# Sorting 400,000 edges to their nodes: first segments of 2 and 6 chunks, both folded beside a third of 66

## The chip, the core and the metric

The kernel runs on one core of a Trainium2 chip. The metric is the device time of one execution in microseconds (us), smaller is better. Before the change the median of three runs is 4207.56 us (4206.01 to 4213.95).

## What is computed

A graph has 12,500 nodes (64 features each) and 400,000 edges (32 features each). Each edge belongs to one source node. Per node the kernel needs the sum, the maximum and the mean of its edges' features; then a small network of two layers runs on them and its result is added to the node's own features. Cut to that:

```python
seg_sum = jax.ops.segment_sum(edge_attr, row, num_segments=N)
seg_max = jax.ops.segment_max(edge_attr, row, num_segments=N)
cnt = jax.ops.segment_sum(jnp.ones((edge_attr.shape[0], 1)), row, num_segments=N)
seg_mean = seg_sum / jnp.maximum(cnt, 1.0)
seg_max = jnp.where(cnt > 0, seg_max, 0.0)
h = jnp.concatenate([seg_sum, seg_max, seg_mean, u[batch]], axis=1)
return x + (jax.nn.relu(h @ W1 + b1) @ W2 + b2)
```

`row` (called `src` in the kernel) is drawn at random, so a node's edges lie anywhere in the list.

## The kernel before

**Chunks and groups.** The edges lie as 128 partitions by 3125 columns. 25 columns are a chunk (125 chunks), 5 columns a group (5 groups in a chunk, 625 in all). One indirect DMA on POOL (line 439) sends one column, 128 edge rows of 128 bytes, to their places in a DRAM array `sorted_rows`; so there are 3125 of them.

**Planes and ranks.** `sorted_rows` is made of planes. A plane has one row for each node (12,544 rows of 128 bytes, 1568 KB). The first edge of a node in a segment goes to the segment's first plane (rank 0), the second to the next one, and so on. Planes have to hold zeros before edges are sent to them; each is zeroed by one DMA (`fill`, line 309), 110 in all. The rank of every edge comes out of matmuls: TensorE compares the edges of a column with one another and keeps a running count (lines 460, 473, 476, 500, 504, 506), ScalarE copies between PSUM and SBUF (lines 615, 623, 636, 638), VectorE builds the one-hot matrices (line 721), picks each edge's rank out (line 730) and writes `position` (line 742), on which POOL waits. The DVE writes the position of a group only when the same group of the chunk before has been sent (`edges_sent`), so it can be about one chunk ahead of POOL and no further.

**Segments.** `SEGMENTS` lists (chunks, ranks, parts). The chunks are cut into six segments with planes of their own. When all edges of a segment are sent, its planes are *folded*: read back as windows of 14 blocks of nodes (two halves of 7 blocks), summed over the ranks by TensorE (`sum_ranks`, line 531, one f32 matmul for each rank and half) and reduced to their maximum by VectorE (`raise_half` and `take_ranks`: line 779 makes a mask of ranks that a node does not have, line 784 adds it, 4 times in a chunk, line 801 takes the maximum rank by rank). There are 7 windows (`ROUNDS`), and a segment's ranks may be cut into parts; each window and part is worked on beside one chunk of the next segment. So 36 ranks in 3 parts are 21 chunks with 12 ranks each, and in the program a loop of 7 turns with a body of 3 chunks. Segments of 1 part are a loop of 7 turns with one chunk each. The last segment is folded at the end, with nothing beside it.

**Order.** `run_chunks` (line 283) lays the same order out for each engine: for each segment some lead chunks, then the chunks with a fold beside them, then the rest. The lead is 3 chunks on TensorE, ScalarE and VectorE and 1 on SP. In its chunk SP issues in this order: for each of the 5 groups the load of the group's edge features (`load_group`, 80 KB, line 313), after waiting until the same group of the chunk before was sent; behind it the plane fills that the chunk has; behind groups 2 and 4 a window half (`load_half`, line 319), after waiting that TensorE and VectorE are done with the half before (lines 359 and 360). All of these go through one hardware queue, first in, first out.

**What POOL waits for.** For each group: `position_ready` and `edges_loaded` of that group. At the start of segments 0 to 3: that the planes which the segment can reach are zeroed (`first_filled`, 8 planes, ahead of everything; `early_filled`, 18 planes, ahead of chunk 4; `middle_filled`, 48, ahead of chunk 17; `late_filled`, 36, ahead of chunk 74). Chunk 0 has no fills, chunks 1 to 17 have 6 each.

```python
SEGMENTS = [(4, 8, 1), (13, 14, 1), (57, 36, 3), (24, 18, 2), (17, 15, 1), (10, 12, 1)]
```

If a node had more edges in a segment than it has ranks, the whole would be done a second time for the edges left over (`passes_i`).

Of the kernel before, what the change touches and what calls it, by code (L numbers as in the profile page):

```python
# [17 lines left out]
SEGMENTS = [(4, 8, 1), (13, 14, 1), (57, 36, 3), (24, 18, 2), (17, 15, 1), (10, 12, 1)]  # L18
BLOCKS = 98
# [5 lines left out]
FILLS = 6  # L25
FILL_CHUNKS = 17
PLANES = BASE[1] + FILLS * FILL_CHUNKS
assert BASE[-1] <= PLANES


def build(nc, x, src, edge_attr, u, w1, b1, w2, b2, out, rows):
# [24 lines left out]
    EARLY, MIDDLE, REMAIN = 3 * FILLS, 8 * FILLS, 6 * FILLS  # L56
# [9 lines left out]
    for s in range(1, SEGS):  # L66
        assert SEGMENTS[s][0] >= LEAD + ROUNDS * parts[s - 1]

    assert first[1] == 4 and first[1] + 1 + ROUNDS * parts[0] <= 13 and first[2] == 17
# [12 lines left out]
    PAIRS = ROUNDS * sum(parts)  # L82
    last_steps = 4 + len(levels(depth[LAST]))
# [10 lines left out]
    with ctx:  # L94
# [46 lines left out]
        left_t = sb("left_t", [P, BLOCKS], FP32)  # L141
# [135 lines left out]
        def pair_at(s, q, r, j):  # L277

            return (s, q * PAIRS + (r * parts[s] + (pair_base[s] + j)), r * 2, j * depth[s],
                    q * STEPS + (r * (parts[s] * pair_steps[s]) + (step_base[s] + j * pair_steps[s])))  # L280

        def run_chunks(eng, q, lead, chunk):


            for s in range(SEGS):
                a, z = first[s], first[s + 1]
                ahead = lead if s > 0 else 1
                for c in range(a, a + ahead):
                    chunk(q * CHUNKS + c, c, c * GROUPS, s, None)
                a += ahead  # L290
                if s > 0:
                    k = parts[s - 1]
# [11 lines left out]
        def _(sp):  # L304
# [27 lines left out]
            with sp.Fori(0, end) as q:  # L332
# [9 lines left out]
                def chunk(c, at, n, s, pair):  # L342
                    done = early_filled if s == 0 else \
                        middle_filled if s == 1 and (n is not None or pair is not None) else \
                        late_filled if s == 1 or (s == 2 and (n is not None and n < (FILL_CHUNKS + 1) * GROUPS)) else None
                    if n == 0:
                        done = None
                    for k in range(GROUPS):
                        if n != 0:
                            sp.wait_ge(edges_sent[k], c * (16 * GROUP))  # L350
                        load_group(c, at, k)
                        if done is not None:
                            fill(at * FILLS + (BASE[1] - FILLS + k), done)
                            if k == GROUPS - 1:
                                fill(at * FILLS + (BASE[1] - 1), done)
                        if pair is not None and k in (2, 4):
                            of, p, f, r, _ = pair
# [89 lines left out]
        def _(pe):  # L447
# [5 lines left out]
            with pe.Fori(0, end) as q:  # L453
# [70 lines left out]
                def sum_ranks(pair, h, a, z):  # L524
                    s, p, _, _, _ = pair
                    if a == 0:
                        pe.wait_ge(win_loaded[h], p * 16 + 16)
                        pe.wait_ge(left_step, q * (3 * SEGS) + (3 * s + 3))
                        pe.wait_ge(sum_folded, p * 2 + (h + 2))
# [158 lines left out]
        def _(dve):  # L688
# [28 lines left out]
            with dve.Fori(0, end) as q:  # L717
# [28 lines left out]
                def take_counts(s):  # L746
                    done = q * (3 * SEGS) + 3 * s
                    dve.wait_ge(count_turned, q * SEGS + (s + 1))
                    nc.vector.tensor_scalar(left_t[:, :], count_ps, -float(BASE[s]), None, ALU.add).then_inc(left_step, 1)
                    dve.wait_ge(left_step, done + 1)  # L750
                    nc.vector.tensor_tensor(left_sum[:, :], left_sum[:, :], left_t[:, :], ALU.add)
                    nc.vector.reduce_max(most_s[:, :], left_t[:, :], axis=AXIS_X).then_inc(left_step, 1)
# [23 lines left out]
                def raise_part(s, h, col, r, a, z, steps):  # L776
# [3 lines left out]
                                            left_t[:, bass.ds(col, SLOTS)].unsqueeze(1).to_broadcast([P, z - a, SLOTS]),  # L780
# [45 lines left out]
                def chunk(c, at, n, s, pair):  # L826
                    for g in range(GROUPS):
                        if pair is not None and g in (2, 4):
                            _, p, f, _, _ = pair
# [5 lines left out]
                        of, p, f, r, steps = pair  # L835
# [108 lines left out]
```

## Time and profile before

| | us |
|---|---|
| median of three runs | 4207.56 (4206.01 to 4213.95) |
| the profiled execution, its own time | 4215.91 |
| its span | 4214.1 |
| POOL busy | 3051.1 (72%) |
| TensorE matmul / VectorE / ScalarE busy | 2943.5 / 2484.8 / 1832.9 |
| moved by DMA | 454.49 MB, 108 GB/s over the span |

The span in 40 slices of 105 us, busy tenths of each engine, the granted TensorE clock in tenths of full speed, and what the DMA engines moved:

```profile
PE   5676668876666666666666677778776777768746
DVE  5466448853333333333333378888875777658876
POOL 5777777777777777777777777777777777777720
PEclk8578558865555555555555588888877888768867
GB/s 296 335 378 380 344 263 117 118 26 26 25 26 25 26 26 25 26 25 26 26 25 26 64 112 117 106 113 109 111 60 78 92 85 94 56 92 123 91 117 100
```

The first six slices are those with plane fills. Slices 7 and 8 have the fold of segment 1, slices 23 to 29 that of segment 2, 31 to 35 that of segment 3, 36 to 38 that of segment 4; the last two are the last fold and the network. POOL shows the same digit throughout: it issues its indirect DMAs one behind the other, and what it needs between two of them is not counted as busy.

### The profile page before, as it was taken

The page shows a single profiled execution, that of the slowest core. Times are in us where ns is not written, and L with a number is a line of the kernel's source. Part 1 is how long each engine was busy: PE and PEld are TensorE (multiplying, and loading weights), DVE is VectorE, ACT ScalarE, POOL GpSimd, SP SyncE. Part 2 cuts the span into 40 slices and gives each one's busy share as a digit, 9 for nine tenths or more (in the row PEclk, how much of TensorE's full clock was granted, in tenths as well). Part 3 has the DMA queues.
Part 4 walks back from the last instruction along what each step waited for, and adds up shares of the span by engine and source line. Part 5 has one row for each costly group of instructions (what it writes and reads, how often), then busy time and mean ns, then how long its engine had stood idle before and what let it go on. Part 6 is the DMA issues. An engine that isn't in the chain of part 4 may idle for free.

```text
span 4214.1 us, 86474 instructions
## 1 busy us (share of the span) xinstructions
PE 2943.5 (70%) x19960; PEld 2213.6 (53%) x19960; DVE 2484.8 (59%) x10168; ACT 1832.9 (43%) x5899; POOL 3051.1 (72%) x3143
## 2 busy tenths in 40 slices
PE   5676668876666666666666677778776777768746
PEld 3455446654444444444444466666665665556635
DVE  5466448853333333333333378888875777658876
ACT  4444443454444444444444444444444444443424
POOL 5777777777777777777777777777777777777720
PEclk8578558865555555555555588888877888768867
DMA  7899874311111111111111234333322333234333
GB/s 296 335 378 380 344 263 117 118 26 26 25 26 25 26 26 25 26 25 26 26 25 26 64 112 117 106 113 109 111 60 78 92 85 94 56 92 123 91 117 100
DMA packets 410045, 454.49 MB, mean 108 GB/s; under 512 B 65002, under 2 KB 381460, under 8 KB 409620
## 3 DMA queue, kind: packets, MB, share of 16 engines
q1 hardware_dynamic: 309876, 401.37, 29.0%
q0 software_dynamic: 100000, 51.40, 5.0%
q14 instruction: 128, 1.05, 0.1%
q8 instruction: 41, 0.67, 0.1%
HBM read 221.50 MB, written 231.02 MB: 107 GB/s over the span
## 4 chain that ended last, share of the span: by engine, by line
POOL 47%; issue 21%; DVE 12%; PE 10%; DMA 7%; ACT 1%; POOLq 1%; SPq 1%; DVEq 1%; ACTq 0%
POOL sorted_rows L439 47%; DVE peak_ps L801 4%; DMA sorted_rows<-edges,position 4%; PE misc_ps L531 3%; DVE raised L784 3%; DMA edges<-in_edge_attr 2%; PE start_ps L500 2%; PE place_ps L504 1%; DVE picked L730 1%; PE same_ps L473 1%; PE place_ps L506 1%; DVE hot_owner L721 1%; DVE raised L812 1%; ACT start_sb L615 1%; PE same_ps L476 1%
## 5 line engine op out<-in xcount | busy, mean ns | idle before, releaser
L439 POOL DMA_INDIRECT sorted_rows<-edges,position x3125 | 3042.3, 974 | 983.0 <-issue 968.7
L504 PE MATMUL place_ps<-start_sb,lent 98*128 98x128 bf16 x3125 | 857.2, 274 | 979.4 <-DVE rank_f L730 978.0
L615 ACT ACTIVATE start_sb<-start_ps 98x128 bf16<-98x128 f32 x3125 | 867.5, 278 | 1207.9 <-PE place_ps L506 586.5
L730 DVE CUSTOM_DVE_ANT_0 picked<-place_ps,hot_owner 128x128 bf16<-128x128 f32 x3125 | 864.5, 290 | 407.9 <-PE place_ps L506 353.1
L500 PE MATMUL start_ps<-hot_owner,hot_block 128*98 128x128 bf16 x3125 | 942.7, 302 | 178.5 <-ACT start_sb L615 134.9
L504 PEld LDWEIGHTS place_ps<-start_sb,lent 98*128 98x128 bf16 x3125 | 391.1, 125 | 1075.4 <-DVE rank_f L730 1056.9
L506 PE MATMUL place_ps<-hot_owner,lent 128*128 128x128 bf16 x3125 | 870.7, 279 | 0.0
L500 PEld LDWEIGHTS start_ps<-hot_owner,hot_block 128*98 128x98 bf16 x3125 | 469.9, 150 | 756.9 <-ACT start_sb L615 639.9
L742 DVE SCALAR_TENSOR_TENSOR position<-rank_c,src_f 128x5 int32<-128x5 f32 x625 | 104.3, 167 | 1188.3 <-DMA sorted_rows<-edges,position 1148.7
L476 PE MATMUL same_ps<-lent 98*128 98x128 bf16 x3125 | 702.4, 283 | 0.0
L636 ACT ACTIVATE lent<-hot_t_ps 98x256 bf16<-98x256 bf16 x625 | 239.6, 383 | 1027.5 <-PE hot_t_ps L460 1025.0
L531 PE MATMUL misc_ps<-win,ident_f 128*128 128x224 f32 x2548 | 641.4, 410 | 0.0
L460 PE MATMUL hot_t_ps<-ident_b,hot_block 128*98 128x128 bf16 x3125 | 619.2, 273 | 24.2 <-DVE hot_owner L721 23.3
L531 PEld LDWEIGHTS misc_ps<-win,ident_f 128*128 128x128 f32 x2548 | 556.9, 228 | 18.8
L623 ACT ACTIVATE lent<-same_ps 128x512 bf16<-128x512 f32 x1250 | 541.7, 433 | 0.3
L473 PE MATMUL same_ps<-later_b,ident_b 128*128 128x512 bf16 x1250 | 515.8, 413 | 0.0
L460 PEld LDWEIGHTS hot_t_ps<-ident_b,hot_block 128*98 128x98 bf16 x3125 | 411.9, 167 | 35.3 <-DVE hot_owner L721 24.4
L476 PEld LDWEIGHTS same_ps<-lent 98*128 98x128 bf16 x3125 | 387.5, 133 | 0.8 <-issue 0.8
L506 PEld LDWEIGHTS place_ps<-hot_owner,lent 128*128 128x128 bf16 x3125 | 386.2, 124 | 0.0
L784 DVE SCALAR_TENSOR_TENSOR raised<-peak_ps,win 128x1344 f32<-128x1344 f32 (+2 forms) x252 | 376.3, 1493 | 8.7
L801 DVE TENSOR_TENSOR peak_ps<-raised,peak_ps 128x448 f32<-128x448 f32 x525 | 329.8, 628 | 16.2
L721 DVE TENSOR_TENSOR hot_owner<-owner,iota_b 128x640 bf16<-128x640 bf16 x625 | 305.5, 489 | 0.0
(80 smaller groups left out, 1725.5 us busy)
## 6 DMA issues: line engine op xcount, KB each, us to landing
sorted_rows<-zeros SPq DMA_DIRECT2D x110, 1568.0 KB, 17.3
win<-sorted_rows SPq DMA_DIRECT2D x56, 1344.0 KB
edges<-in_edge_attr SPq DMA_DIRECT2D x625, 80.0 KB
sorted_rows<-edges,position POOLq DMA_INDIRECT x3125
win<-sorted_rows SPq DMA_DIRECT2D x28, 1008.0 KB
win<-sorted_rows SPq DMA_DIRECT2D x14, 1680.0 KB
win<-sorted_rows SPq DMA_DIRECT2D x14, 1568.0 KB
win<-sorted_rows SPq DMA_DIRECT2D x14, 896.0 KB
```

What stands on the lines that cost most here:

```text
L439: nc.gpsimd.indirect_dma_start(out=rows[:, :], out_offset=bass.IndirectOffsetOnAxis(ap=position[:, t:t + 1], axis=0), in_=edges[:, k, j * ...
L460: last = nc.tensor.transpose(hot_t_ps[0:BLOCKS, j * P:(j + 1) * P], hot_block[:, slot * GROUP + j, :], ident_b[:, :])
L473: nc.tensor.matmul(same_ps[:, a * P:z * P].rearrange("p (j m) -> p j m", m=P), ident_b[:, :], later_b[:, :].unsqueeze(1).to_broadcast([P, ...
L476: last = nc.tensor.matmul(same_ps[:, j * P:(j + 1) * P], hot, hot, start=False, stop=j in (BANK_TILES - 1, GROUP - 1), skip_group_check=True)
L500: nc.tensor.matmul(start_ps[0:BLOCKS, 0:P], hot_block[:, t, :], hot_owner[:, t, :], start=False, stop=False, skip_group_check=True).then_i ...
L504: nc.tensor.matmul(place_slot(j), hot_block_t[:, slot, j * P:(j + 1) * P], start_sb[:, j, :], start=True, stop=False)
L506: nc.tensor.matmul(place_slot(j), earlier[:, slot, j * P:(j + 1) * P], hot_owner[:, t, :], start=False, stop=True).then_inc(place_ready, 1)
L531: last = nc.tensor.matmul(side_sums[h], ident_f[:, :], win[:, h, r, :], start=(r == 0), stop=(r == depth[s] - 1))
L615: nc.scalar.activation(start_sb[:, j, :], start_ps[0:BLOCKS, 0:P], ACT.Copy)\
L623: nc.scalar.activation(earlier[:, slot, a * P:z * P], same_ps[:, a * P:z * P], ACT.Relu)\
L730: nc.vector.tensor_tensor_reduce(out=picked[:, j, :], in0=place_slot(j), in1=hot_owner[:, t, :], scale=1.0, scalar=0.0, op0=ALU.mult, op1= ...
L784: return nc.vector.scalar_tensor_tensor(raised[:, h, a:z, :].rearrange("p r (b f) -> p r b f", f=FEAT), mask.unsqueeze(3).to_broadcast([P, ...
```

## The change

It does four things. (1) The first segments get 2 chunks with 6 ranks and 6 chunks with 9, and the third 66 chunks with 39 ranks, 13 in each of its 3 parts; segments 3 to 5 begin at the same chunks as before (74, 98, 115) with the same ranks. (2) Nothing is folded beside segments 0 and 1. Both are folded beside segment 2: segment 0 beside chunks 9 to 15 and segment 1 beside chunks 16 to 22 in SP's order, two chunks later on the others; for this the count table `left_t` gets two buffers. (3) Chunks 0 to 7 have 7 fills each, the first of them in chunk 0 right behind its edge loads; chunks 8 to 15 have 6 each. (4) The waits follow: 6 planes ahead of everything, 14 more ahead of chunk 2, 42 more ahead of chunk 8, 48 ahead of chunk 74. There are 110 fills as before. The ranks to fold are 99 instead of 103.

```diff
-SEGMENTS = [(4, 8, 1), (13, 14, 1), (57, 36, 3), (24, 18, 2), (17, 15, 1), (10, 12, 1)]
+SEGMENTS = [(2, 6, 1), (6, 9, 1), (66, 39, 3), (24, 18, 2), (17, 15, 1), (10, 12, 1)]
+
+BESIDE = [[], [], [0, 1], [2], [3], [4]]
...
-FILLS = 6
-FILL_CHUNKS = 17
-PLANES = BASE[1] + FILLS * FILL_CHUNKS
-assert BASE[-1] <= PLANES
+FILLS = (7, 6)
+FILL_CHUNKS = (8, 8)
+PLANES = BASE[1] + FILLS[0] * FILL_CHUNKS[0] + FILLS[1] * FILL_CHUNKS[1]
+assert BASE[-1] - 1 <= PLANES
...
-    EARLY, MIDDLE, REMAIN = 3 * FILLS, 8 * FILLS, 6 * FILLS
+    EARLY, MIDDLE, REMAIN = 2 * FILLS[0], 6 * FILLS[0], 8 * FILLS[1]
...
-        left_t = sb("left_t", [P, BLOCKS], FP32)
+        left_t = sb("left_t", [P, 2, BLOCKS], FP32)
...
-                ahead = lead if s > 0 else 1
+                ahead = lead if BESIDE[s] else 1
...
-                if s > 0:
-                    k = parts[s - 1]
+                for of in BESIDE[s]:
+                    k = parts[of]
                     with eng.Fori(0, ROUNDS) as r:
                         for j in range(k):
-                            chunk(q * CHUNKS + (r * k + (a + j)), r * k + (a + j), None, s, pair_at(s - 1, q, r, j))
+                            chunk(q * CHUNKS + (r * k + (a + j)), r * k + (a + j), None, s, pair_at(of, s, q, r, j))
...
                     for k in range(GROUPS):
                         if n != 0:
                             sp.wait_ge(edges_sent[k], c * (16 * GROUP))
                         load_group(c, at, k)
-                        if done is not None:
-                            fill(at * FILLS + (BASE[1] - FILLS + k), done)
-                            if k == GROUPS - 1:
-                                fill(at * FILLS + (BASE[1] - 1), done)
+                        for i in range(k, fills, GROUPS):
+                            fill(at * fills + (base + i), done)
...
                 def turn_counts(s):
-                    if s > 0:
-                        pe.wait_ge(sum_folded, q * (PAIRS * 2) + (pair_base[s] * 2 + 2))
+                    if pairs_before[s] > 0:
+                        pe.wait_ge(sum_folded, q * (PAIRS * 2) + (pairs_before[s] * 2 + 2))
```

SP at the start of the program. `zeros` are the plane fills, `in_edge_attr` the edge loads of chunk 0. Before:

```order
L309 DMA sorted_rows<-zeros 256x1x1568 x8
L313 DMA edges<-in_edge_attr 128x160 x5
L298 UNCONDITIONAL_BRANCH
L298 ISA
L313 ISA
```

And now:

```order
L313 DMA sorted_rows<-zeros 256x1x1568 x6
L317 DMA edges<-in_edge_attr 128x160
L313 DMA sorted_rows<-zeros 256x1x1568 x2
L317 DMA edges<-in_edge_attr 128x160
L313 DMA sorted_rows<-zeros 256x1x1568 x2
L317 DMA edges<-in_edge_attr 128x160
L313 DMA sorted_rows<-zeros 256x1x1568
L317 DMA edges<-in_edge_attr 128x160
L313 DMA sorted_rows<-zeros 256x1x1568
L317 DMA edges<-in_edge_attr 128x160
L313 DMA sorted_rows<-zeros 256x1x1568
```

Two fills fewer stand ahead of the first edge load, and two stand between the first and the second, and between the second and the third.

VectorE in a chunk with a fold of segment 2 beside it, the two instruction pairs of one half of a window (mask, then mask and window to `raised`). Before:

```order
L784 SCALAR_TENSOR_TENSOR raised<-peak_ps,win 128x1344
L792 REGISTER_ALU
L779 TENSOR_TENSOR peak_ps<-left_t,iota_f 128x42
L783 REGISTER_ALU
L784 SCALAR_TENSOR_TENSOR raised<-peak_ps,win 128x1344
```

And now:

```order
L785 SCALAR_TENSOR_TENSOR raised<-peak_ps,win 128x1344
L793 REGISTER_ALU
L780 TENSOR_TENSOR peak_ps<-left_t,iota_f 128x49
L784 REGISTER_ALU
L785 SCALAR_TENSOR_TENSOR raised<-peak_ps,win 128x1568
```

The second of the two is one rank (224 elements) longer; behind them one more maximum of 128x448 (line 801, now 802) is taken in each chunk, 12 where there were 11, and TensorE adds up 13 ranks of each half where there were 12.

## Rows read from the trace of the kernel before

**Rows 1.** The page, its line of busy engines (us, share of the span).

```profile
PE 2943.5 (70%) x19960; PEld 2213.6 (53%) x19960; DVE 2484.8 (59%) x10168; ACT 1832.9 (43%) x5899; POOL 3051.1 (72%) x3143
```

**Rows 2.** Page, group of line 439; POOL's timeline (start, us): first two, last.

```profile
L439 POOL DMA_INDIRECT sorted_rows<-edges,position x3125 | 3042.3, 974 | 983.0 <-issue 968.7
...
41.14 1.12 POOL L439 DMA_INDIRECT sorted_rows<-edges,position  x1 [31.55 <-issue]
42.57 0.96 POOL L439 DMA_INDIRECT sorted_rows<-edges,position  x1 [0.30 <-issue]
...
4033.93 0.96 POOL L439 DMA_INDIRECT sorted_rows<-edges,position  x1 [0.30 <-issue]
```

**Rows 3.** Stretches: PE, PEld, DVE, ACT, POOL busy, clock, DMA share, GB/s.

```profile
10.00:34.00 24.00, 9.42 (x63) 7.00 (x63) 17.69 (x30) 12.31 (x22) 0.00 (x0) 1.00 1.02 423
300.00:400.00 100.00, 70.16 (x518) 55.26 (x516) 68.90 (x268) 42.86 (x140) 75.94 (x79) 0.85 1.02 381
1000.00:1100.00 100.00, 65.51 (x430) 45.45 (x431) 39.53 (x224) 44.72 (x142) 75.94 (x80) 0.52 0.11 26
```

**Rows 4.** Start: SP's fills, the chain's last fill to landing, DVE's first position.

```profile
4.74 12.37 SPq L309 DMA_DIRECT2D sorted_rows<-zeros  x8
...
13.35 26.43 DMA sorted_rows<-zeros
...
33.59 0.17 DVE L742 SCALAR_TENSOR_TENSOR position<-rank_c,src_f 128x5 int32<-128x5 f32 x1
```

**Rows 5.** The page's DMA issues (size of each).

```profile
sorted_rows<-zeros SPq DMA_DIRECT2D x110, 1568.0 KB, 17.3
...
edges<-in_edge_attr SPq DMA_DIRECT2D x625, 80.0 KB
...
win<-sorted_rows SPq DMA_DIRECT2D x14, 896.0 KB
```

**Rows 6.** Chain: an edge load, issue to landing; POOL's first DMA of chunk 12.

```profile
402.67 15.52 DMA edges<-in_edge_attr
...
423.65 0.96 POOL L439 DMA_INDIRECT sorted_rows<-edges,position  x1 [0.30 <-issue]
```

**Rows 7.** Stretches of line 742 alone: start:end, length, busy (x positions), clock, DMA.

```profile
2438.20:3121.54 683.34, 17.54 (x105) 0.84 0.37 107
2633.92:2729.42 95.50, 2.54 (x15) 0.88 0.39 113
2923.62:3022.60 98.98, 2.48 (x15) 0.81 0.38 110
661.58:866.35 204.77, 5.12 (x30) 0.83 0.37 107
3788.02:3994.12 206.10, 5.01 (x30) 0.88 0.38 113
```

**Rows 8.** From the start: positions made (line 742), indirect DMAs issued (line 439).

```profile
0.00:2438.30 2438.30, 63.44 (x381) 0.60 0.35 116
0.00:3090.10 3090.10, 80.10 (x481) 0.65 0.35 115
...
0.00:2461.00 2461.00, 1841.24 (x1901) 0.61 0.34 116
0.00:3102.30 3102.30, 2330.22 (x2401) 0.65 0.35 114
```

**Rows 9.** SP's timeline, the issues ahead of chunk 96.

```profile
3084.24 0.38 SPq L319 DMA_DIRECT2D win<-sorted_rows  x1
3085.12 6.83 SPq L313 DMA_DIRECT2D edges<-in_edge_attr  x3
```

**Rows 10.** ScalarE's timeline at the top of the loop of 3 chunks.

```profile
2635.92 0.28 ACT L615 ACTIVATE start_sb<-start_ps 98x128 bf16<-98x128 f32 x1 [2.98 <-issue]
```

**Rows 11.** DVE groups in 2460 to 3100 us, by form.

```profile
L801 DVE TENSOR_TENSOR peak_ps<-raised,peak_ps 128x448 f32<-128x448 f32 x198 | 124.4, 628 | 6.1
L784 DVE SCALAR_TENSOR_TENSOR raised<-peak_ps,win 128x1344 f32<-128x1344 f32 x78 | 121.5, 1558 | 2.7
```

More of the change, by code:

```diff
@@ L66, in build @@
     for s in range(1, SEGS):
-        assert SEGMENTS[s][0] >= LEAD + ROUNDS * parts[s - 1]
-    assert first[1] == 4 and first[1] + 1 + ROUNDS * parts[0] <= 13 and first[2] == 17
+        assert SEGMENTS[s][0] >= LEAD + ROUNDS * sum(parts[j] for j in BESIDE[s])
+    assert first[1] == 2 and first[2] == 8 and SP_LEAD + ROUNDS * parts[0] == 8
+    assert BASE[2] - 1 <= BASE[1] + EARLY and BASE[3] - 1 <= BASE[1] + EARLY + MIDDLE
     DEPTH = max(depth)
@@ L82, in build @@
     PAIRS = ROUNDS * sum(parts)
+    pairs_before = [ROUNDS * sum(parts[j] for k in range(s + 1) for j in BESIDE[k]) for s in range(SEGS)]
     last_steps = 4 + len(levels(depth[LAST]))
@@ L275, in end_pass, with pair_at @@
             eng.sem_inc(pass_seen, 1)
-        def pair_at(s, q, r, j):
-            return (s, q * PAIRS + (r * parts[s] + (pair_base[s] + j)), r * 2, j * depth[s],
+        def pair_at(s, host, q, r, j):
+            return (s, host, q * PAIRS + (r * parts[s] + (pair_base[s] + j)), r * 2, j * depth[s],
                     q * STEPS + (r * (parts[s] * pair_steps[s]) + (step_base[s] + j * pair_steps[s])))
@@ L342, in chunk @@
                 def chunk(c, at, n, s, pair):
[L343 to L347, printed above, removed]
+                    done, fills, base = (early_filled, FILLS[0], BASE[1]) if s == 0 else \
+                        (middle_filled, FILLS[0], BASE[1]) if s == 1 else \
+                        (late_filled, FILLS[1], BASE[1] + (FILLS[0] - FILLS[1]) * FILL_CHUNKS[0]) \
+                        if s == 2 and (n is not None or (pair is not None and pair[0] == 0)) else (None, 0, 0)
                     for k in range(GROUPS):
@@ L351, in chunk @@
                         load_group(c, at, k)
-                        if done is not None:
-                            fill(at * FILLS + (BASE[1] - FILLS + k), done)
-                            if k == GROUPS - 1:
-                                fill(at * FILLS + (BASE[1] - 1), done)
+                        for i in range(k, fills, GROUPS):
+                            fill(at * fills + (base + i), done)
                         if pair is not None and k in (2, 4):
-                            of, p, f, r, _ = pair
+                            of, _, p, f, r, _ = pair
                             h = k // 2 - 1
@@ L524, in sum_ranks @@
                 def sum_ranks(pair, h, a, z):
-                    s, p, _, _, _ = pair
+                    s, host, p, _, _, _ = pair
                     if a == 0:
                         pe.wait_ge(win_loaded[h], p * 16 + 16)
-                        pe.wait_ge(left_step, q * (3 * SEGS) + (3 * s + 3))
+                        pe.wait_ge(left_step, q * (3 * SEGS) + 3 * host)
                         pe.wait_ge(sum_folded, p * 2 + (h + 2))
@@ L748, in take_counts @@
                     dve.wait_ge(count_turned, q * SEGS + (s + 1))
-                    nc.vector.tensor_scalar(left_t[:, :], count_ps, -float(BASE[s]), None, ALU.add).then_inc(left_step, 1)
+                    nc.vector.tensor_scalar(left_t[:, s % 2, :], count_ps, -float(BASE[s]), None, ALU.add).then_inc(left_step, 1)
                     dve.wait_ge(left_step, done + 1)
-                    nc.vector.tensor_tensor(left_sum[:, :], left_sum[:, :], left_t[:, :], ALU.add)
-                    nc.vector.reduce_max(most_s[:, :], left_t[:, :], axis=AXIS_X).then_inc(left_step, 1)
+                    nc.vector.tensor_tensor(left_sum[:, :], left_sum[:, :], left_t[:, s % 2, :], ALU.add)
+                    nc.vector.reduce_max(most_s[:, :], left_t[:, s % 2, :], axis=AXIS_X).then_inc(left_step, 1)
                     dve.wait_ge(left_step, done + 2)
@@ L779, in raise_part @@
                     nc.vector.tensor_tensor(mask,
-                                            left_t[:, bass.ds(col, SLOTS)].unsqueeze(1).to_broadcast([P, z - a, SLOTS]),
+                                            left_t[:, s % 2, bass.ds(col, SLOTS)].unsqueeze(1).to_broadcast([P, z - a, SLOTS]),
                                             iota_f[:, r + a:r + z].unsqueeze(2).to_broadcast([P, z - a, SLOTS]),
@@ L828, in chunk @@
                         if pair is not None and g in (2, 4):
-                            _, p, f, _, _ = pair
+                            _, _, p, f, _, _ = pair
                             h = g // 2 - 1
@@ L834, in chunk @@
                             continue
-                        of, p, f, r, steps = pair
+                        of, _, p, f, r, steps = pair
                         col, half = f * SLOTS, depth[of] // 2
```

## The prediction

> **What bounds the kernel now.** I read the busy engines first, then POOL's own timeline, then stretches of it, and last what stands ahead of POOL at its start and in the folds. POOL is busy 72% [rows 1], no more than TensorE, but its indirect DMAs have 0.96 us each and 0.30 us of issue between two, and nothing else: the first starts at 41.14, the last at 4033.93 [rows 2]. That is 3992.8 us for 3124 steps, 1.278 each. A quiet stretch has 79 or 80 of them in 100 us [rows 3], so 1.267 each, 6.33 a group, 31.7 a chunk, and 3124 such steps would be 3958. POOL never stalls for long: the 35 us over that are DMAs somewhat longer than 0.96 us beside folds, and one at the end. So the time is 41.1 of start, 3993 of POOL, and 180 us behind its last DMA (last fold, network). A change counts if it moves POOL's first DMA, makes POOL stall, or alters the tail. All else is cover, and the question is how thick the cover is.
>
> **Terms.** The sum is made against the profiled execution (4215.91, span 4214.1), which is 8.35 above the median of the runs; I put the difference onto the median.
>
> *The start.* POOL waits for the planes of segment 0, its first edge load and its first position. The eighth fill lands at 13.35 + 26.43 = 39.78 [rows 4], and POOL starts 1.36 later; I take 1.1 of that for the wake, the edge load of 80 KB [rows 5] landing in between at about 40.0. While only fills run, 423 GB/s are moved [rows 3], so a plane of 1568 KB (1.606 MB) [rows 5] takes 3.80. Six planes are in place at 39.78 - 7.60 = 32.2, the first load at 32.4, which would let POOL go at 33.5. The first position is written at 33.59 to 33.76 [rows 4], so it now comes last, and POOL starts at about 34.0. **-7.1.**
>
> *Fills between the edge loads of chunk 0.* The queue is first in, first out. The second load stands two planes behind the first: 2 x 3.80 + 0.3 = 7.9, landing 40.3, usable 41.4, and POOL wants it at 34.0 + 6.33 = 40.3: it stalls 1.1. For the third there are two planes again, now beside POOL's rows. In the busiest stretch the queue moves 381 GB/s [rows 3], a plane in 4.21: 8.6 more, usable at 50.0, wanted at 47.7: 2.3. Behind the fourth and fifth only one plane each, 4.4 against 6.33: no stall. **+3.4** (nothing at least, if the queue overlaps more; 5 at most). The Trainium skill, "DMA: Bandwidth & Descriptors", section "Where 436 GB/s comes from", gives 435 GB/s as the ceiling of the fabric. By that a plane is an estimated 3.7 us throughout, the term 2.1 and the sum 10.0 instead of 11.3; the trace reaches 423 with fills alone but 381 once rows and windows are in the mix, and I go by the trace.
>
> *Chunks 1 to 15.* A chunk with 7 fills moves 7 x 1.606 + 0.41 of edges in + 0.41 of rows out = 12.06 MB, at 381 GB/s 31.7 us: just POOL's pace. Before, the chunks with a fold of 8 ranks beside 6 fills moved 9.63 + 1.84 (two halves of 896 KB [rows 5]) + 0.82 = 12.29 MB, 32.3 us, and what was left at their end was this: a load issued at 402.67 landed at 418.19 and its chunk's first DMA started at 423.65 [rows 6], 5.5 us of slack, still no stall. The new chunks 9 to 15 (6 fills, 6 ranks) move 11.8 MB. The backlog therefore stays, but doesn't grow. The 14 early planes: 8 of the first 20 are done by 39.8, 12 x 4.21 and 10 loads (2 us) end at about 92.4, and POOL reaches chunk 2 at 34.0 + 63.4 + 3.4 = 100.8. The 42 next ones end 190 us later, at about 282, chunk 8 starts at 291. **0** (0 to +3). What covers this is 8 us; if it goes, POOL stalls by what is missing, and once only.
>
> *Folds of segments 0 and 1*, 6 and 9 ranks a chunk where 8 and 14 were. The one with 14 took 204.77 / 6 = 34.1 us a chunk on the DVE [rows 7] against POOL's 32.0 and ate the lead for 7 chunks, but never all of it. Less work there gives nothing. **0.** The folds as a whole have 4 ranks fewer, and that is hidden too.
>
> *The fold of segment 2*, 21 chunks, 13 ranks instead of 12. This is the large term. Look at who is ahead of whom. The 381st position (chunk 76, first group) is written by 2438.3, and POOL's DMA 1901, which uses it, starts just before 2461.0 [rows 8]: a lead of 22.5. The 481st (chunk 96) is written by 3090.1, DMA 2401 starts just before 3102.3: 12.0. Ten microseconds went in 20 chunks: the DVE needs 683.34 / 21 = 32.54 a chunk there [rows 7], POOL 32.07 (641.4 for 20). The edge loads are as close: SP sits behind its wait for TensorE, issues a window half of 12 ranks (1.5 times the 896 KB [rows 5] of 8 ranks) at 3084.24 and only then the loads for chunk 96 [rows 9], which land some 5 us later, about 3090.5; less 1.1 of wake some **10 us** are left.
>
> What does one more rank cost a chunk? In itself on the DVE: one maximum, 0.63 and a gap of 0.03, and one rank in each half of `raised`, 2 x 1.558 / 6 = 0.52 [rows 11]: 1.18. The DVE is in the chain in these steps, so little of it hides. From whole chunks: with 14 ranks 34.13, with 15 ranks 206.10 / 6 = 34.35, in loops of one chunk. The 12-rank loop has a body of 3, and at its top ScalarE loses 2.98 us that nothing shown explains [rows 10], 1.0 a chunk; the one-chunk loops have no such gap. So 12 ranks are 32.54 - 1.0 = 31.54 and a rank is (34.13 - 31.54) / 2 = 1.30. Bounds: without that correction 0.80; against the quickest turns, 95.50 / 3 - 1.0 = 30.8, it is 1.66. I take 1.25, between the two that agree. In 20 chunks 25 us are wanted and 10 are there: **POOL stalls 15 us** in the last third of the fold (ends: 6 and 23). When the fold is over the lead is rebuilt, but what POOL has lost stays lost, because POOL is the bound.
>
> *Segments 3 to 5 and the tail*: same chunks, ranks and code. **0.** The 15-rank fold keeps its thin lead.
>
> Sum: -7.1 + 3.4 + 0 + 15 = **+11.3**. On the median 4218.9.
>
> **Rivals.**
>
> *The clock favours the new fold.* Same code, same ranks: a turn of three chunks takes 95.50 at a granted clock of 0.88 and 98.98 at 0.81 [rows 7]. Which level a turn gets is not fixed by the program's text: three of the seven were quick. If all seven were quick with 13 ranks: 95.5 + 3.75 = 99.3 against POOL's 96.2, 3.0 a turn, 21 us for a lead of 19 to 22: stall 0 to 2. Then -7.1 + 3.4 + 1 = -2.7, **4204.9**, not slower: this is the case on the other side, and it decides at about 99.0 us a turn. For it: the 15-rank fold ran at 0.88 throughout; against it: the 14-rank fold had 0.83 with more ranks than 12. The Trainium skill, "TensorE: Matmul & The Clock Gate", section "Part 1: The HAM clock gate", says that the default is throttled and activity releases it; by it one more f32 matmul in each half speaks for this rival, the rows above only for half of it. Chance 0.27.
>
> *The slow clock throughout.* 99.0 + 3.75 = 102.7, 6.5 a turn, 46 in seven less 19: stall 26, **4230**. Chance 0.12.
>
> *The queue is the bound in the first chunks.* If 7 fills a chunk take 32.3 us as the heaviest chunks of before, each of chunks 1 to 7 adds up to 0.6 behind a cover that chunk 0 has used up: +4 on top of the forecast, 4223. For it: the DMA share is 1.02 already [rows 3]. Chance 0.08.
>
> *It gains its start and nothing is taken back.* A rank hides altogether, and the loads of chunk 0 come in time: -7.1, **4200.5**. Chance 0.05. *It doesn't do what it says*: a node with more edges than ranks would cost a second pass, some 4000 us. In the reference's draw the fullest node has 5, 8 and 37 edges in the three new segments, for 6, 9 and 39 ranks. Chance nil.
>
> **Numbers.** Forecast (stall between 8 and 22) 0.48. A measurement of this kernel tells about 0.2% from no change, 8.4 us: faster is below 4199.1, slower above 4216.0. Within the forecast a stall under 12.1 us still reads as no change, a quarter of it: slower 0.36 + 0.12 + 0.08 = 0.56, same 0.12 + 0.27 + 0.02 = 0.41, faster 0.03, the start's gain with a fortunate clock. The range goes from the case without a stall, 4200, to the upper bound of a rank with the queue's 3 us, 4207.6 - 3.7 + 23 + 3 = 4230, and some way into the slow clock with it: 4235. The likeliest case's own range is 4212 to 4226.
>
> **What would show it.** Right: POOL's first DMA near 34, DMA 26 (chunk 1) near 69 instead of 73.4; gaps of some us in POOL's row only between 2850 and 3130; turns of three chunks on the DVE of 99 to 103 us; SP's loads of those chunks landing as POOL wants them. Wrong: turns of 99 or less and POOL without gaps (a rank hides, or the clock); POOL's chunk 1 at 73 (the fills ate the start); gaps before 300 us (the queue); another length behind POOL's last DMA than 180.

## The result, and the profile after

The changed kernel takes 4232.07 us (median of five runs, 4230.23 to 4238.99) against 4207.56: a ratio of 1.0061, 95% interval 1.0049 to 1.0073, or 24.5 us more. The forecast had been 4218.9 (11.3 us more) in a range of 4200 to 4235. So the sign and the range held, but less than half of the rise was forecast, and 4232 lies above the likeliest case's own range of 4212 to 4226. The profiled execution took 4231.62 with a span of 4229.2, on its own median.

The page of the changed kernel: its busy engines, the moved GB/s in 40 slices of 105.7 us, the shares of the chain by engine, POOL's group (us in all, mean ns | idle time before) and the plane fills (KB each, median us from issue to landing).

```profile
PE 2943.9 (70%) x19848; PEld 2210.3 (52%) x19848; DVE 2448.5 (58%) x10140; ACT 1834.1 (43%) x5899; POOL 3038.8 (72%) x3143
...
GB/s 394 390 375 370 365 94 94 36 25 26 26 25 26 26 26 25 26 26 25 26 26 26 85 112 110 109 108 109 113 80 75 94 85 94 55 91 124 91 120 97
...
POOL 45%; issue 20%; DVE 11%; DMA 11%; PE 9%; ACT 1%; POOLq 1%; SPq 1%; DVEq 1%; ACTq 0%
...
L440 POOL DMA_INDIRECT sorted_rows<-edges,position x3125 | 3029.9, 970 | 1010.0 <-issue 964.9
...
sorted_rows<-zeros SPq DMA_DIRECT2D x110, 1568.0 KB, 14.7
```

The busy times tell nothing: VectorE's fell by 36 us [rows 1] while the kernel became 24.5 slower, and POOL's group is 12 us less busy and 27 us more idle [rows 2]. One has to look at where POOL stood idle. POOL's timeline (start, duration, in brackets the idle time before it): start, the third group of chunk 0, the last DMA ahead of the first stall beside the fold and the one behind it, a stall one turn later, and the last DMA.

```profile
34.78 1.12 POOL L440 DMA_INDIRECT sorted_rows<-edges,position  x1 [25.21 <-issue]
...
50.28 0.96 POOL L440 DMA_INDIRECT sorted_rows<-edges,position  x1 [2.83 <-issue]
...
2755.62 0.96 POOL L440 DMA_INDIRECT sorted_rows<-edges,position  x1 [0.30 <-issue]
2759.89 0.96 POOL L440 DMA_INDIRECT sorted_rows<-edges,position  x1 [3.31 <-DMA edges<-in_edge_attr]
...
2865.21 0.95 POOL L440 DMA_INDIRECT sorted_rows<-edges,position  x1 [3.21 <-DMA edges<-in_edge_attr]
...
4048.57 0.96 POOL L440 DMA_INDIRECT sorted_rows<-edges,position  x1 [0.30 <-issue]
```

Between the two profiled executions the 15.1 us of span come together like this (each rounded), taken from the starts of POOL's first DMA of a chunk: start -6.4 (41.14 to 34.78), chunk 0 +2.5 (32.3 to 34.8), chunks 1 to 15 +2.3, chunks 16 to 24 -2.3 (288.9 to 286.6), the quiet chunks 25 to 73 -6.0 (1556.5 to 1550.5), chunks 74 and 75 -0.3, **the 21 chunks beside the fold of segment 2 +25.1** (673.5 to 698.6), all later chunks together -0.4 and the tail +0.5. The -2.3 and most of the -6.0 belong to that one execution of before, not to the change: another profile of before has 286.2 in chunks 16 to 24 and 1553.0 in the quiet ones. The quiet chunks take 1550.3 to 1554.1 in eleven of the twelve profiles of the experiments and 1557.5 in the last. With the other profile's values in these two stretches the sum is +21.3, near the +24.5 of the medians; what makes the last 2.5 us of the quiet chunks is not known.

The fold of segment 2 on VectorE: two turns of three chunks and all seven, then the quiet chunks (start:end, length, busy PE, PEld, DVE, ACT, POOL, granted clock, DMA share, GB/s).

```profile
2528.88:2631.87 102.99, 80.26 (x563) 65.60 (x562) 83.84 (x279) 41.54 (x135) 78.28 (x82) 0.83 0.38 111
2631.87:2734.14 102.27, 78.55 (x565) 64.29 (x563) 83.57 (x279) 41.60 (x136) 77.88 (x81) 0.85 0.38 113
...
2427.99:3147.19 719.20, 560.00 (x3921) 458.09 (x3921) 587.24 (x1953) 290.56 (x942) 526.04 (x542) 0.83 0.37 108
...
836.40:2386.90 1550.50, 1010.56 (x6618) 698.53 (x6618) 606.51 (x3434) 693.20 (x2206) 1177.00 (x1225) 0.53 0.11 26
```

719.2 where before had 683.3 [rows 7], 102.7 a turn for 97.6. The lead of a position over the DMA that uses it was 22.6 us at chunk 76, and then at every third chunk 17.2, 9.6, 3.3, 1.6, 2.6, 2.6, 2.0; before it was 22.5 and still 12.6 at chunk 97. The bookkeeping closes: 719.2 less the 20.6 us of lead used up is 698.6, what POOL took. What POOL waited for in that stretch (us in total, times, longest), after the change and then before it:

```profile
POOL sorted_rows L440 <- issue: 155.1, 494, 1.5
POOL sorted_rows L440 <- DMA edges<-in_edge_attr: 23.2, 12, 3.4
POOL sorted_rows L440 <- DVE position L743: 10.0, 19, 2.0
```

```profile
POOL sorted_rows L439 <- issue: 157.8, 518, 0.3
POOL sorted_rows L439 <- DVE position L742: 1.2, 4, 0.3
POOL sorted_rows L439 <- DMA edges<-in_edge_attr: 1.2, 4, 0.3
```

The edge load ends the longer waits, 23.2 us in 12, and the position more of them, 10.0 us in 19. It isn't the DMA engines that are short (share 0.37): SP issues these loads behind its wait until TensorE and VectorE are done with a window half. In the trace it is TensorE's sum that ends this wait (493 us in 39 waits), but the sum stands between steps that VectorE sets the pace of: below, a rank less on TensorE changes nothing and a rank less on VectorE takes the loss away. And at the top of each turn VectorE now stands still for no reason that the trace names:

```profile
2845.04 0.29 DVE L731 CUSTOM_DVE_ANT_0 picked<-place_ps,hot_owner 128x128 bf16<-128x128 f32 x1 [5.39 <-issue]
```

It does so for 5.3 to 5.8 us six times, once at each return to the loop's head. Before, ScalarE had 2.7 to 3.5 us of this kind there [rows 10]. VectorE stood still at the same instruction then too, for 3.1 to 3.3 us, but behind ScalarE: it waited for TensorE, which waited for ScalarE. A gap of its own of that length would not show:

```profile
2732.92 0.29 DVE L730 CUSTOM_DVE_ANT_0 picked<-place_ps,hot_owner 128x128 bf16<-128x128 f32 x1 [3.33 <-PE place_ps L506]
```

### The profile page after: what moved, and what is told of

Read it like the earlier page. It is cut to its first block, busy times and chain, and to the rows that moved or that the text cites. A ratio compares the mean times of both kernels' runs of the same rounds, so it can differ in the third digit from the quotient of the medians.

```text
span 4229.2 us, 86184 instructions
## 1 busy us (share of the span) xinstructions
PE 2943.9 (70%) x19848; PEld 2210.3 (52%) x19848; DVE 2448.5 (58%) x10140; ACT 1834.1 (43%) x5899; POOL 3038.8 (72%) x3143
## 4 chain that ended last, share of the span: by engine, by line
POOL 45%; issue 20%; DVE 11%; DMA 11%; PE 9%; ACT 1%; POOLq 1%; SPq 1%; DVEq 1%; ACTq 0%
POOL sorted_rows L440 45%; DMA edges<-in_edge_attr 7%; DMA sorted_rows<-edges,position 4%; DVE peak_ps L802 4%; PE misc_ps L532 3%; DVE raised L785 2%; PE start_ps L501 2%; DVE picked L731 1%; PE place_ps L505 1%; DVE hot_owner L722 1%; PE same_ps L474 1%; PE place_ps L507 1%; DVE raised L813 1%; ACT start_sb L616 1%; PE same_ps L477 1%
## 5 line engine op out<-in xcount | busy, mean ns | idle before, releaser
L532 PEld LDWEIGHTS misc_ps<-win,ident_f 128*128 128x128 f32 x2436 | 545.0, 233 | 20.4
L785 DVE SCALAR_TENSOR_TENSOR raised<-peak_ps,win 128x1344 f32<-128x1344 f32 (+3 forms) x252 | 363.2, 1441 | 8.7
L802 DVE TENSOR_TENSOR peak_ps<-raised,peak_ps 128x448 f32<-128x448 f32 x497 | 312.2, 628 | 15.2
```

What stands on the lines that cost most here:

```text
L532: last = nc.tensor.matmul(side_sums[h], ident_f[:, :], win[:, h, r, :], start=(r == 0), stop=(r == depth[s] - 1))
L802: nc.vector.tensor_tensor(peak, raised[:, :, r, :], prior, ALU.max).then_inc(unit_step, 1)
```

## The experiments

Two theories stood at first. **A**: the 13th rank makes VectorE's turns longer, the lead of 20 us is used up, and then POOL stalls by the whole difference. **B**: what costs is the changed program's loop top with its new gap of 5.4 us. What each expects of a run is quoted ahead of its result. Ratios are to the kernel before on the same chip.

### The old cut with the new depth

```diff
-SEGMENTS = [(4, 8, 1), (13, 14, 1), (57, 36, 3), ...]
+SEGMENTS = [(4, 8, 1), (13, 13, 1), (57, 39, 3), ...]
```

(an edit of the kernel before; segment 1 has a rank less, so that the planes suffice)

> The kernel before with 39 ranks in its third segment (57 chunks, 13 ranks in each part) and 13 in its second; everything else as before. Theory A (one rank more in each of 21 chunks is the loss, with the DVE's gap at the top of the loop belonging to a longer body): turns of three chunks near 102.5 us, POOL loses about 25 us in chunks 82 to 97, +25 on before. Theory B (the gap of 5.5 us at the loop's top comes from where the changed program's loops lie in memory, not from the ranks): gap 0 to 3 us, turns near 100, POOL loses 5 to 12. Theory C (the new cut itself, not the ranks, is the loss): nothing against before.

Measured: 4230.95, ratio 1.0056 (1.0042 to 1.0070). The loss is there without any of the new cut. A turn, all turns, and ScalarE at a loop top:

```profile
2738.00:2840.39 102.39, 80.33 (x561) 65.75 (x561) 84.01 (x280) 41.52 (x135) 74.70 (x77) 0.83 0.38 113
...
2434.46:3147.60 713.14, 561.82 (x3921) 459.77 (x3921) 588.57 (x1953) 289.83 (x942) 523.42 (x540) 0.84 0.37 110
```

```profile
2638.38 0.28 ACT L615 ACTIVATE start_sb<-start_ps 98x128 bf16<-98x128 f32 x1 [3.52 <-issue]
```

VectorE has no gap of 5.4 here (at the loop's top it stands still for 3.2 to 4.0 us, behind ScalarE as before), yet its turns come to 713.1, and POOL needs 695.2 for the 21 chunks. That is 21.7 more than before with nothing changed beside the fold but the rank: A, with 6 us of VectorE's time left for B. Two of the seven turns are quick ones (99.9 and 99.8 at clocks of 0.88 and 0.86); the changed kernel has none of under 100.9.

### One rank of each part left out

```diff
-    depth = [w // k for w, k in zip(ranks, parts)]
+    stride = [w // k for w, k in zip(ranks, parts)]
+    depth = [d - 1 if s == 2 else d for s, d in enumerate(stride)]
```

(an edit of the changed kernel, as all others where nothing else is said; `pair_at` steps by `stride`)

> The changed kernel, but of the 13 ranks of each part of the third segment only 12 are loaded, summed and maximised (ranks 12, 25 and 38 are left out). Theory A: turns back to 95.5 to 99 us, no gap of 5.5 us on the DVE at the loop's top, no stall of POOL, so 23 to 27 less than the changed kernel, near 4207. Theory B: the gap stays at about 5.5, turns 98 to 101.5, a stall of 5 to 10, so only about 17 less.

Measured: 4206.65, ratio 0.9997 (0.9988 to 1.0006).

```profile
2625.74:2724.67 98.93, 76.53 (x551) 62.07 (x549) 80.78 (x276) 41.57 (x136) 75.44 (x78) 0.85 0.37 109
...
2428.38:3124.08 695.70, 545.74 (x3837) 442.67 (x3837) 566.10 (x1933) 290.22 (x942) 526.06 (x541) 0.83 0.36 105
```

With the rank goes the whole loss, as A has it: POOL takes 676.4 for the 21 chunks. But the gap at the loop's top stays, as B has it (5.1 to 5.4), and with 12 ranks the turns are still 99.4 on average, 1.8 above before, so the lead falls to 3.2 and POOL stalls about 4 us beside the fold. The rank costs (719.2 - 695.7) / 21 = 1.12 a chunk here, where 1.25 had been taken.

### The parts one after the other

```diff
-                    with eng.Fori(0, ROUNDS) as r:
-                        for j in range(k):
-                            chunk(..., r * k + (a + j), ..., pair_at(of, s, q, r, j))
+                    for j in range(k):
+                        with eng.Fori(0, ROUNDS) as r:
+                            chunk(..., r + (a + j * ROUNDS), ..., pair_at(of, s, q, r, j))
```

Three loops of seven chunks with a body of one, instead of one loop with a body of three; same work.

> The changed kernel with the folds of 3 and of 2 parts run part by part: three loops of 7 turns with one chunk in the body instead of one loop with three. Same work, other order. If the loop's top costs time only with a long body (2.98 on ScalarE before, 5.5 on the DVE after): three chunks near 99, POOL loses 0 to 5 instead of 25, 20 to 25 less than the changed kernel. If the rank alone is the loss: three chunks stay near 102, no difference.

Measured: 4209.85, ratio 1.0009 (1.0000 to 1.0018): of the loss of 0.61% 0.09% is left, with all 13 ranks still in. A turn and all of them:

```profile
2730.05:2829.14 99.09, 80.50 (x564) 66.05 (x562) 83.92 (x279) 41.53 (x136) 75.31 (x79) 0.84 0.39 116
...
2428.18:3129.40 701.22, 570.64 (x3921) 467.66 (x3921) 589.43 (x1953) 289.80 (x942) 525.90 (x543) 0.83 0.38 111
```

No gap of the kind on any engine; 18.0 us off VectorE's seven turns at an unchanged clock of 0.83, and POOL takes 679.8. So the loop's form costs too, as B has it, and not only the rank.

### All edge loads of chunk 0 ahead of its fills

```diff
-                        for i in range(k, fills, GROUPS):
+                        for i in range(k, fills, GROUPS) if n != 0 else range(fills) if k == GROUPS - 1 else ():
```

> The changed kernel, but the 7 fills of chunk 0 are issued behind all five of its edge loads instead of between them. If the queue's order is what stalls POOL in chunk 0: the gap of 2.5 us at POOL's tenth DMA goes, POOL reaches chunk 1 at 66.5 instead of 69.6, 2 to 3 less in all. If the queue is the bound for all of chunks 0 to 7, the time comes back as a stall later, at the third group of chunks 1 to 7: 0 to 1 less.

Measured: 4231.45, ratio 1.0057 (1.0043 to 1.0071). Chunk 1 begins at 66.9 instead of 69.6, and then POOL's timeline has this (DMAs 31 and 36 of all):

```profile
73.93 0.96 POOL L440 DMA_INDIRECT sorted_rows<-edges,position  x1 [0.98 <-issue]
...
82.52 0.96 POOL L440 DMA_INDIRECT sorted_rows<-edges,position  x1 [2.58 <-issue]
```

Chunk 2 begins at 101.7 as before the edit. The stall of chunk 0 only moved: by that the queue is the bound in chunks 0 and 1, whichever of the two stands first in it.

### Whose work is the 13th rank

TensorE sums one rank less, VectorE does all 13:

```diff
+    summed = [d - 1 if s == 2 else d for s, d in enumerate(depth)]
...
-                                                stop=(r == depth[s] - 1))
+                                                stop=(r == summed[s] - 1))
```

> The changed kernel, where TensorE adds up 12 of the 13 ranks of a part (rank 12, 25, 38 left out of the sum) and VectorE does all 13. If the DVE's 1.2 us a chunk is what the rank costs: turns stay at 102 to 103, the time at 4229 to 4233. If TensorE's two f32 matmuls are: turns near 99, about 20 less.

Measured: 4238.16, ratio 1.0065 (1.0050 to 1.0081).

```profile
2431.59:3152.53 720.94, 546.14 (x3837) 444.03 (x3837) 588.12 (x1954) 291.00 (x942) 526.62 (x543) 0.83 0.37 108
```

And the other way round, in `raise_half`, `take_ranks` and `keep_peak`:

```diff
+    raised_of = [d - 1 if s == 2 else d for s, d in enumerate(depth)]
...
-                    raise_part(s, h, col, r, half, depth[s], steps + 2).then_inc(win_raised, 1)
+                    raise_part(s, h, col, r, half, raised_of[s], steps + 2).then_inc(win_raised, 1)
```

> The changed kernel, where VectorE raises and maximises 12 of the 13 ranks of a part (ranks 12, 25, 38 left out of the maximum) and TensorE adds up all 13. If the DVE is what the rank costs: turns near 99 as with the rank left out on both, POOL loses 3 to 6, the time near 4208. If it is TensorE: turns stay above 101.5, the time above 4224.

Measured: 4205.92, ratio 0.9989 (0.9980 to 0.9998); POOL's 21 chunks take 673.0, no more than before.

```profile
2429.86:3120.28 690.42, 551.47 (x3921) 451.02 (x3921) 561.96 (x1933) 288.11 (x942) 522.76 (x540) 0.85 0.38 113
```

TensorE's thirteenth matmul costs nothing (720.9 without it, 719.2 with it). VectorE's part is all of it: 28.8 us in 21 chunks, 1.37 each. The clock was 0.85 with 13 matmuls and 12 maxima and 0.83 in the other three mixes (one profile of each), so the matmul may do it some good, as the Trainium skill has it ("TensorE: Matmul & The Clock Gate", "Part 1: The HAM clock gate"); VectorE's extra work takes that back.

### The kernel before once more

> The kernel before once more, for its profile. If quick turns (95.5 us of three chunks) belong to its code: at least two of seven again, and POOL loses nothing in chunks 76 to 97 (672 to 675 us). If they were chance: turns of 98 to 100, a lead that falls below 8 us, and the quiet chunks 25 to 74 shorter than the 1556.5 us of the first profile (1550 to 1553 as in all later ones).

One run, 4213.93. Quick and slow turns are there again, four quick ones of seven:

```profile
2725.58:2824.19 98.61, 79.90 (x549) 64.69 (x549) 81.24 (x276) 41.49 (x135) 75.14 (x78) 0.81 0.38 110
...
2920.15:3015.83 95.68, 73.20 (x549) 59.61 (x549) 80.23 (x276) 41.64 (x135) 73.09 (x75) 0.87 0.39 113
```

All seven are 678.2, POOL 672.3, the lead never under 15 at the turns' starts.

### A cut that keeps the early start with 36 ranks

```diff
-SEGMENTS = [(2, 6, 1), (6, 9, 1), (66, 39, 3), (24, 18, 2), ...]
+SEGMENTS = [(2, 6, 1), (6, 9, 1), (62, 36, 3), (28, 20, 2), ...]
-FILLS = (7, 6)
+FILLS = (6, 6)
```

with the parts one after the other, one fill behind each edge load and the sixth behind the last.

> A version meant to keep the early start and lose nothing: first segments as changed, the third 62 chunks with 36 ranks in 3 parts, the fourth 28 chunks with 20 ranks in 2 parts, parts run one behind the other with one chunk in each loop's body, and 6 fills in chunks 0 to 15, one behind each edge load and the sixth behind the fifth. Start at 34 to 35, no stall in chunk 0, chunks 0 to 8 at 31.7, three chunks of the fold at 93 to 96, no stall there: 6 to 7 less than before, 4199 to 4201. If 20 ranks beside the fifth segment or the one-chunk loops cost something, 4203 to 4210.

Measured: 4202.59, ratio 0.9980 (0.9970 to 0.9991); on another chip, the same kernel:

> The kernel of 62 chunks with 36 ranks, part by part, once more on whatever chip comes: if its first result (0.998 of before) holds, 0.997 to 0.999 again; if that was the chip, as much as its two halves made on another one (0.9992 and 0.9993).

4196.65 against 4207.15, ratio 0.9973 (0.9963 to 0.9983). What POOL waited for from its start to beyond the fold, in that second run:

```profile
POOL sorted_rows L441 <- issue: 778.6, 2472, 25.2
POOL sorted_rows L441 <- DMA edges<-in_edge_attr: 3.0, 10, 0.3
POOL sorted_rows L441 <- DVE position L744: 2.4, 8, 0.3
```

POOL starts at 33.9 and 34.8, chunk 0 takes 32.5 and 32.3, and there is no stall: a kernel faster than both, 9.5 and 10.5 us below the kernel before, where 6 to 7 had been expected. To see which half of it does that, the two halves were run apart. The kernel before with its parts one after the other:

> The kernel before with its folds of 3 and 2 parts run part by part (one chunk in each loop's body). Three chunks of the DVE take 93 to 97 us instead of 95.5 to 99 and the lead in front of POOL stays above 15 us. POOL loses nothing in that fold in either kernel, so if a lead that isn't used up is worth nothing, the time is before's within 0.1%. If a quicker fold helps POOL by itself: 5 or more less.

4203.73, ratio 0.9993 (0.9983 to 1.0002); VectorE's turns are 675.1, POOL's chunks 668.3. That is 4 to 5 us less than in the two profiles of before (673.5 and 672.3), in which POOL did not stall either; how the order of the parts reaches POOL there no run shows. And the new cut with the loop of three chunks:

> The kernel of 62 chunks with 36 ranks and 6 fills a chunk, with the loops of 3 and 2 chunks as in the changed kernel. If the ranks of a chunk are what the change had to keep: 12 ranks, turns of 95.5 to 99 (101 if the DVE's gap at the loop's top is there), POOL loses 0 to 4, the time 4200 to 4206 on a chip where before has 4207. If the part-by-part order made the gain: 4208 or more.

4203.47, ratio 0.9992 (0.9983 to 1.0001). Two turns:

```profile
2531.83:2630.74 98.91, 76.60 (x552) 62.11 (x550) 80.66 (x277) 41.57 (x136) 75.13 (x79) 0.85 0.37 110
2630.74:2732.30 101.56, 80.75 (x552) 65.43 (x550) 80.92 (x277) 41.47 (x136) 77.17 (x81) 0.80 0.36 106
```

The gap of 5.1 to 5.4 is back, the six whole turns average 99.7 instead of 96.8, the lead falls to 1.3, and POOL stalls some 5 us. Neither half alone is told from no change; the two together are.

### The same loop at another place in the stream

```diff
+        def spend(a, z):
+            for i in range(a, z):
+                nc.vector.tensor_scalar(spare[:, i:i + 1], iota_f[:, 0:1], 1.0, None, ALU.add)
...
+                if s == 3:
+                    spend(pad // 2, pad)
...
+                if s == 2:
+                    spend(0, pad // 2)
```

(on VectorE only, `pad` = 235)

> The changed kernel with 235 tiny instructions more on VectorE (one 128x1 write each into a tile that nothing reads), 117 ahead of the quiet loop of segment 2 and 118 ahead of the lead chunks of segment 3, where VectorE is idle most of the time. Nothing else is different; the fold's loop of three chunks has the same 498 instructions on VectorE, but begins at the 1711th of its stream instead of the 1476th, which is where it begins with the old cut and 39 ranks (no such gap there). ScalarE's loop, without a gap of its own in the changed program, stays where it is. Theory A, the place of the loop in the instruction stream decides whether its jump back finds its target at hand: the gap of 5.1 to 5.8 us at the loop's top goes (under 1.5), turns fall from 102.7 to 100 to 101.5, POOL's chunks 76 to 97 take 678 to 690 instead of 698.6, time 4208 to 4222, ratio 1.001 to 1.004. Theory B, the gap comes from what the changed loop contains or from its neighbours in the program: it stays at 5.1 to 5.8, turns 102.7, ratio 1.005 to 1.007.

Measured: 4231.32 against 4215.43 on that chip, ratio 1.0037 (1.0023 to 1.0050). VectorE at a loop's top, one turn, and all of them:

```profile
2740.34 0.29 DVE L741 CUSTOM_DVE_ANT_0 picked<-place_ps,hot_owner 128x128 bf16<-128x128 f32 x1 [3.28 <-issue]
```

```profile
2637.41:2736.89 99.48, 76.76 (x562) 62.92 (x561) 83.45 (x279) 41.39 (x135) 75.72 (x79) 0.88 0.39 114
...
2433.98:3145.54 711.56, 566.18 (x3921) 462.93 (x3921) 588.72 (x1953) 290.39 (x942) 527.12 (x543) 0.83 0.37 110
```

Neither theory had this: the gap did not go, nor did it stay. It was 5.3 to 5.8 us and is 3.28 to 3.38, at all six tops. The loop has the same instructions; only its distance from the program's start is another. So its place changes the gap's size. The loop begins where it begins with the old cut and 39 ranks, and there VectorE stood still for 3.2 to 4.0 us at this instruction, behind ScalarE: the expectation took that for no gap, but the same gap can have lain hidden in it. VectorE's turns came down by 7.6 us (the six gaps together by 13), to what the old cut with 39 ranks has (713.1), and a quick turn is back. POOL takes 690.3, 0.3 above the 678 to 690 of theory A, on a chip where its quiet chunks took 1557.5, longer than in any other profile. The ratio lies within theory A's 1.001 to 1.004.

## Why the prediction was right in kind and short in size

**The bound** was read rightly. The time follows POOL's row in all kernels, and what moved with the edits was its start and its stalls.

**The start**: -7.1 forecast, -6.4 measured. The position of the first group now ends the wait, as the term had it; in the profiles POOL goes at 33.9 or 34.8 with the same program.

**Fills between the loads of chunk 0**: +3.4 forecast, +2.5 measured, by another split. The third group stalled 2.5 (2.3 forecast), the second, for which 1.1 was forecast, not at all.

**Chunks 1 to 15**: forecast 0, with up to 3 in the range. Measured +2.3 against the first profile of before and +1.9 against the second. The rival in which the queue is the bound was right about the place: moving chunk 0's fills changed nothing, chunk 2 starts at 101.7 either way. It had the price too high, 4 us on top.

**Folds of segments 0 and 1, the rest and the tail**: 0, as forecast.

**The fold of segment 2**: +15 forecast, +25.1 measured, above the term's own upper end of 23. This is the step that failed, and it is one term of it. The lead was right: 20 us of it was there to be used. It was gone sooner than forecast: the first stall came at 2757 and not behind 2850, all of them before 3130. That it is VectorE's work was right, and the price of a rank nearly: 1.12, 1.37 and 1.42 a chunk by three subtractions against 1.25, and 1.24 between the two kernels with one chunk in the body ((701.2 - 675.1) / 21), where no gap blurs it. Forecast and measured VectorE time are 709.6 and 719.2, and the forecast of POOL's stall is short by about that difference. Of these 9.6 us, 7.6 went away when the same loop stood 235 instructions further on; with it there POOL's 21 chunks took 690.3, a stall of 16.8 over before. The sum of 15 was thus the price of the rank, and what it left out was that the **change moves the fold's loop in VectorE's instruction stream**, where VectorE stands still for 5.4 us a turn at the jump back instead of some 3.3. The order of instructions had been read for what stands in the loop, not for where the loop stands. [rows 10] had shown such a gap, on ScalarE, and the working used it only to set 1.0 us a chunk apart.

The average turns tell it in one table (us a turn, whole turns of the fold):

| loop of the fold | 12 ranks | 13 ranks |
|---|---|---|
| one chunk in the body, no gap | 96.4, 96.8 | 100.2 |
| three chunks, about 3 us (VectorE or ScalarE) | 97.6, 96.9 | 101.9, 101.7 |
| three chunks, 5.4 us on VectorE | 99.4, 99.7 | 102.7, 102.9, 103.0 |

From the first row to the last the loop's form costs 2.5 to 3.3 us, and along a row the rank costs 3.0 to 5.0. The rank in loops of one chunk, or the long gap with 12 ranks, fits into the lead almost whole (ratios 0.9992 to 1.0009). With before's own loop and its 3 us the rank alone already brings 21.7 of the 25.1 us. In the changed kernel the two together exceed the lead: 5.1 us more a turn is 36 in seven turns against a spare lead of some 10 at its end.

**The rivals.** The one in which the slow clock holds throughout, with a chance of 0.12, named the right numbers (turns of 102.7, stall 26, 4230) for a wrong reason. The forecast's own terms reached to 4230 and the range was drawn to 4235 for this case, so it is in part luck that 4232 lies in it. The reason doesn't hold: the fold's granted clock was 0.83 against 0.84 before, and turns at 0.85 took 102.3 where the old slow ones took 98.98 at 0.81. The one in which the clock favours the new fold fell: no turn was quick. The quick turns of before are a part of that program, since they came again, four of seven in the second profile. With 13 ranks and a loop of three chunks they came where the gap was short (99.9, 99.8, 99.5 at 0.86 to 0.88), and once where it was long, with 12 matmuls on TensorE, but in the first turn, ahead of the first jump back (99.8 at 0.88). Why the clock's level and the length of the gap go together isn't settled.

**The profile's own excess.** The profiled execution of before was 8.35 above its median, and against the second profile of before 6.1 us of excess lie in its chunks 16 to 73. So the two profiles differ by only 15.7, near the forecast of 11.3, while the medians differ by 24.5. The smaller number would have looked like a confirmation.

## What to carry to other kernels

Ask of a supporting engine not how busy it is but how far it is ahead, at the beginning and at the end of a stage: added work is free until the lead is used up and counts in full after that, and two harmless additions can be one stall. When a change alters the code ahead of a long loop, the loop's top is part of the change even where its body is the same: look for idle time without a named cause at the first instruction after the jump back, on each engine, and split a long body into several loops of a short one if the engine is near the bound. Compare a stretch that the change doesn't touch before putting the difference of two profiles beside that of two medians.

## What the hardware showed unasked

**The price of a jump back.** VectorE's loop of three chunks has 498 instructions with 13 ranks and 492 with 12. Where it begins at the 1476th instruction of VectorE's stream, the engine stood still at its head for 5.1 to 6.1 us in all six kernels; where the same loop of 498 begins at the 1711th, for 3.3. ScalarE's loop of 331 instructions had 2.7 to 4.1 us in the kernel before and with its old cut, and nothing in the changed kernel, with the same body at another place. Bodies of one chunk on these engines (106 to 174 instructions) had none at any place they stood, nor had VectorE's loops of two chunks (319 and 323) or TensorE's loops of up to 649 (weight loads not counted). The Trainium skill, "Runtime: NRT & Kernel Launch", section "Instruction fetch mechanics", says that most engines hold two blocks of 256 instructions and TensorE four times as many, and that a taken branch to a target outside them has to fetch it first. By that rule (an estimate: two blocks are 512 instructions) a body near 500 fits in only where it begins near a block's start, and one of 331 in most places but not all; the trace agrees in that short bodies and TensorE are free and that place matters. How many blocks were fetched in a gap of 3.3 and in one of 5.4 no run here shows, so why the place changes the length stays open; nor does one show a place at which a body of 492 or 498 had no gap at all, since in the kernel before one of 3 us could hide behind ScalarE's.

**One slow indirect DMA.** In every profile one instruction of POOL's last chunk (number 3111 to 3114) is followed by the next only after 7.4 to 8.8 us instead of 1.27. It was the same in all kernels; no run shows its cause.

**Chips.** The kernel before had medians of 4206.35, 4206.67, 4207.15, 4212.05 and 4215.43 on five chips, a spread of 0.2%, as large as most effects here. Only the ratios to runs on the same chip can be read.
